# A fused WKV, attention and expert kernel: how gates, q and k travel, where v's bias is added, and which step does what

## The reference

```python
tf = sigmoid(sum(time_emb))                       # per batch
# bi-directional WKV along the tokens, as a gate on a hidden state
h1 = bi_wkv(r=x, k=fside, v=fside, w, u, tf)
qkv = h1 @ Wqkv.T + bqkv                          # 16 heads of 16 channels
a = softmax(q @ k.T * scale) @ v
x1 = x + a @ Wproj.T + bproj
h2 = bi_wkv(r=x1, k=fside, v=fside, w2, u2, tf)   # same scans, second decay
score = sigmoid(h2 @ gate_w.T)                    # 64 experts in 8 groups
# best 4 groups, best 6 experts, weights normalised, times 2.5
y = sum_e gate_e * (relu(h2 @ w1_e.T) ** 2) @ w2_e.T
out = x1 + y + (relu(h2 @ shared_up.T) ** 2) @ shared_down.T
```

## Time and profile before

| | us |
|---|---|
| median of 3 runs | 625.95 (624.86 to 629.41) |
| the profiled execution | 627.93 |
| its span on the core | 626.1 |
| TensorE busy in it | 400.3 (64%), granted clock 0.793 on average |
| VectorE, ScalarE, GpSimd busy | 310.4, 203.9, 129.6 |

### The profile page before, as it was taken

How to read it: one execution, slowest core, us unless ns; L and a number is a source line. 1 busy time by engine, 2 the same in 40 slices (tenths; PEclk the granted TensorE clock), 3 DMA queues, 4 the chain that set the end, 5 groups by cost and what they waited for, 6 DMA issues and landing times.

```text
span 626.1 us, 5613 instructions
## 1 busy us (share of the span) xinstructions
PE 400.3 (64%) x1580; PEld 287.2 (46%) x1580; DVE 310.4 (50%) x552; ACT 203.9 (33%) x392; POOL 129.6 (21%) x117
## 2 busy tenths in 40 slices
PE   0526877688725646768985866672756566576664
PEld 0315554555514435546764654451444444454442
DVE  7779566663462332445653538532433434344343
ACT  3224325533503222244652523321232322323232
POOL 5164315120101010123221221210211212112121
PEclk9957567969657777778998976778878878778889
DMA  7792355142670121212322222222222222232221
GB/s 190 105 169 35 35 67 69 22 49 32 130 111 17 60 93 64 75 56 76 105 79 92 78 94 79 93 71 71 93 90 81 78 93 93 78 92 78 92 97 70
DMA packets 33952, 50.91 MB, mean 81 GB/s; under 512 B 3146, under 2 KB 15626, under 8 KB 33930
## 3 DMA queue, kind: packets, MB, share of 16 engines
q1 hardware_dynamic: 33930, 50.65, 33.1%
HBM read 39.16 MB, written 1.33 MB: 65 GB/s over the span
## 4 chain that ended last, share of the span: by engine, by line
DMA 30%; SPq 28%; PE 18%; DVE 11%; issue 7%; ACT 3%; POOL 1%; DVEq 0%; ACTq 0%; POOLq 0%
SPq L305 20%; DMA ex<-gates 17%; SPq L309 5%; DMA q_st<-nmax_lo 5%; DMA clip<-in_tiles 4%; DMA k_st<-qk_lo 3%; PE ps L1188 3%; PE ps L1243 3%; SPq L343 2%; DVE mx L867 2%; DVE scan L814 2%; DVE t_lo L1019 2%; DVE scan L1098 2%; SPq L351 2%; PE ps L1211 2%
## 5 line engine op out<-in xcount | busy, mean ns | idle before, releaser
L483 POOL TENSOR_TENSOR scan<-scan 128x512 f32<-128x512 f32 x68 | 72.8, 1071 | 372.9 <-ACT scan L647 361.0
L1321 PE MATMUL ps<-hid_hi,t_hi 128*128 128x512 f32 x136 | 71.0, 522 | 91.2 <-DVE t_lo L1019 91.2
L1103 DVE TENSOR_TENSOR qk_lo<-scan,qk_hi 128x512 fp32r<-128x512 f32 x68 | 70.4, 1036 | 70.3 <-ACT qk_hi L657 69.4
L1019 DVE TENSOR_TENSOR t_lo<-clip,t_hi 128x512 fp32r<-128x512 f32 x68 | 47.5, 699 | 102.8 <-ACT t_hi L637 102.7
L637 ACT ACTIVATE t_hi<-clip 128x512 fp32r<-128x512 f32 x68 | 42.6, 627 | 155.3 <-DMA clip<-in_tiles 140.4
L1321 PEld LDWEIGHTS ps<-hid_hi,t_hi 128*128 128x128 f32 x136 | 31.0, 228 | 117.6 <-DVE t_lo L1019 59.1
L1098 DVE TENSOR_TENSOR scan<-scan,ex 128x512 f32<-128x512 f32 x68 | 49.5, 728 | 64.6 <-DMA ex<-gates 42.9
L1211 PE MATMUL ps<-k_st,q_st 96*128 96x256 f32 x128 | 37.2, 384 | 61.5 <-DVE mx L867 53.8
L1332 PE MATMUL ps<-qk_hi,t_hi 128*128 128x512 f32 x136 | 64.3, 473 | 7.4 <-DVE qk_lo L1103 7.3
L1323 PE MATMUL ps<-hid_hi,t_lo 128*128 128x512 f32 x136 | 65.4, 481 | 0.0
L1322 PE MATMUL ps<-hid_lo,t_hi 128*128 128x512 f32 x136 | 64.7, 476 | 0.0
(11 more groups left out here) (123 smaller groups left out, 495.1 us busy)
## 6 DMA issues: line engine op xcount, KB each, us to landing
clip<-in_tiles SPq DMA_DIRECT2D x68, 256.0 KB, 14.6
ex<-gates SPq DMA_DIRECT2D x68, 256.0 KB
q_st<-qk_hi SPq DMA_DIRECT2D x16, 128.0 KB, 3.9
q_st<-qk_lo SPq DMA_DIRECT2D x16, 128.0 KB, 4.9
k_st<-qk_hi SPq DMA_DIRECT2D x16, 128.0 KB, 5.9
k_st<-qk_lo SPq DMA_DIRECT2D x16, 128.0 KB, 6.6
f_sb<-in_fT SPq DMA_DIRECT2D x4, 256.0 KB, 8.6
x_sb<-in_xT SPq DMA_DIRECT2D x4, 256.0 KB, 9.4
```

The costliest lines, as they stand in the source:

```text
L483: g.tensor_tensor(sq[:, k], relu[:, k], relu[:, k], ALU.mult).then_inc(sq_ready, 1)
L1103: TT(act_lo[:, k], act[:, k], act_hi[:, k].bitcast(F32), ALU.subtract).then_inc(act_lo_ready, 1)
L1321: mm(bank_h(bank), w_hi, x_hi, start=(c == 0), stop=False)
```

## The change

1. **Gates.** The spread of a unit's two gate rows is two transfers, one for each row and 64 partitions, instead of one whose source is [2, 64, 512].
2. **q and k.** For batches 1 to 3, `store_qk` writes `qk_hi` and `qk_lo` to DRAM (four transfers of 256 KB a batch), and `load_stack` reads the stacks from there: two of 32 rows for q, four of 16 rows for k, in rows of 8 KB. The evacuation of batches 2 and 3 waits for the stores instead of the stacks.
3. **v's bias** goes through the output projection: before the loop TensorE multiplies it by the output weights (`project_bias`, eight matmuls of one column), and the sum with the projection's bias is what `residual` adds. The output weights are loaded earlier.
4. **Steps.** q and k are projected half at a step over two steps (q 1 and 2; k 4 and 5, in batch 2 5 and 6), v over steps 11 and 12 (12 and 13); `hidden1` is at step 0, the scans follow one step earlier; the tails of batches 0 and 1 begin two and one steps later; the first gates of the router are computed at step 10 and at step 0 of the second loop, and it runs at steps 1 to 4. `GAP` is 2, so every unit from 2 on comes one step later. `jobs` is reordered to match.

```diff
-GAP = 1
+GAP = 2
...
+    qk_dram = nc.dram_tensor("qk_split", (2, B, KC, 2, HD, HB * S), F32, kind="Internal").ap()
...
         def values_at(g):
-            return [n // 4 for n in range(3, H * B, 4) if head_slot(n) + 1 == g]
+            return [n // 4 for n in range(3, H * B, 4) if head_slot(n) + (2 if n in (H + 7,) or n == 7 else 1) == g]
 
         def tail_slot(b):
-            return head_slot(H * b + H - 1) + 2
+            return head_slot(H * b + H - 1) + (4, 3, 2, 2)[b]
...
-            sp.dma_start(bvb[:], bv.partition_broadcast(P)).then_inc(ld_w, 16)
+            sp.dma_start(wo[:], w_out).then_inc(ld_wo, 16)
+            sp.dma_start(bvs[:], bv.rearrange("(c p) -> p c", p=P), allow_slow_non_contiguous=True).then_inc(ld_wo, 16)
...
             def load_spread(half, t, k):
 
-                sp.dma_start(spread[:, k], gates[t, :, half * HT:(half + 1) * HT].unsqueeze(1).broadcast_to([2, P // 2, HT])
-                             ).then_inc(ld_spread[k], 16)
+                for r in range(2):
+                    sp.dma_start(spread[r * (P // 2):(r + 1) * (P // 2), k],
+                                 gates[t, r, half * HT:(half + 1) * HT].unsqueeze(0).broadcast_to([P // 2, HT])
+                                 ).then_inc(ld_spread[k], 16)
...
+            def store_qk(b):
+
+                for w in range(2):
+                    for n, (part, ready) in enumerate(((qk_hi, qk_hi_ready), (qk_lo, qk_lo_ready))):
+                        sp.wait_ge(ready, 4 * b + 2 * w + 2)
+                        sp.dma_start(qk_dram[w, b, :, n].rearrange("t d (h s) -> (d h) t s", s=S),
+                                     part[:, w].bitcast(F32)).then_inc(st_qk[w], 16)
+
...
                 for w in range(2):
+                    if b > 0:
+                        sp.wait_ge(st_qk[w], 32 * b)
+                        src = qk_dram[w, b, half]
+                        width = STACK // (2, 4)[w]
+                        for r in range(0, STACK, width):
+                            rows = src.rearrange("n d s -> (n d) s") if w == 0 else src[r // (STACK // 2)]
+                            sp.dma_start((q_st, k_st)[w][r:r + width, n].rearrange("p h s -> p (h s)").bitcast(F32),
+                                         rows).then_inc(ld_stack[n], 16)
+                        continue
...
             for b in range(B - 1):
+                store_qk(b + 1)
                 load_rows(b, 0)
                 load_stack(b + 1, 0)
...
             def evacuate_qk(b, w):
-                if b > 0:
+                if b == 1:
                     for half in range(KC):
-                        sc.wait_ge(ld_stack[slot(b - 1, half)], 128 * turn(b - 1, half))
+                        sc.wait_ge(ld_stack[slot(0, half)], stacked(0, half))
+                if b > 1:
+                    sc.wait_ge(st_qk[w], 32 * (b - 1))
...
-                    if name == "v":
-                        last = mm(job_bank(job)[:, t * S:(t + 1) * S], k_st[MAXROW:MAXROW + 1, 0, 0, 0:P].bitcast(F32),
-                                  bvb[MAXROW:MAXROW + 1, :], start=False, stop=True, skip_group_check=True)
...
+            def project_bias():
+
+                pe.wait_ge(ld_wo, 32)
+                for t in range(KC):
+                    for c in range(KC):
+                        last = mm(ps[:, 4, S + t:S + t + 1], wo[:, c, t * P:(t + 1) * P], bvs[:, c:c + 1],
+                                  start=(c == 0 and t == 0), stop=(c == KC - 1), skip_group_check=True)
+                last.then_inc(bias_ready, 1)
...
-                if s == 2:
-                    project(b + 1, "q")
+                if s in (1, 2):
+                    project(b + 1, "q", s - 1)
                 if s == 3:
                     subtract_high(b + 1, 0)
-                if s == 4:
-                    project(b + 1, "k")
+                if s - (4, 4, 5)[b] in (0, 1):
+                    project(b + 1, "k", s - (4, 4, 5)[b])
...
+                if s - (11, 11, 12)[b] in (0, 1):
+                    project(b + 1, "v", s - (11, 11, 12)[b])
```

More of the change, by code:

```diff
@@ L81, in bass_adaln_attn_ffn @@
         gw = sb("gw", [P, KC, E])
-        bvb = sb("bvb", [P, C])
+        bias = sb("bias", [P, KC])
+        bvs = sb("bvs", [P, KC])
         gbb = sb("gbb", [P, E])
@@ L170, in bass_adaln_attn_ffn @@
         fill_ready, ld_fill = sem("fill_ready"), sem("ld_fill")
+        st_qk = [sem(f"st_qk{w}") for w in range(2)]
         ld_stack = [sem(f"ld_stack{n}") for n in range(SLOTS)]
@@ L258, in unit_bank, with stacked @@
             return n % 2 if n >= ALONE else 1
+        def stacked(b, half):
+            return 96 * turn(b, half) + (32 if slot(b, half) < 2 else 0)
         def unit_at(s):
@@ L388, in _ @@
                 next_spread(n, 0, n, n % RING)
-            for s in range(HB - 1, HEAD + 1):
-                if s + 1 >= 2 * RING and s + 1 < HEAD:
-                    n = s + 1
+            for s in range(HB - 1, HEAD + 2):
+                n = s + RING + 2 - ENTRY - GAP
+                if 2 * RING <= n < HEAD:
                     next_raw(n, n % NT, n % RING)
-                n = s - 1
+                n = s + RING - ENTRY - GAP
                 if n == NT + SHARED:
@@ L652, in round_act @@
                 if isinstance(n, int) and n == 0:
-                    for half in range(KC):
-                        sc.wait_ge(ld_stack[slot(B - 1, half)], 128 * turn(B - 1, half))
+                    for w in range(2):
+                        sc.wait_ge(st_qk[w], 32 * (B - 1))
                 if not isinstance(n, int) or n >= 2:
@@ L1044, in _ @@
             num_den(1, 0, 1)
+            dve.wait_ge(bias_ready, 1)
+            TT(bias[:], ps[:, 4, S:S + KC], vec[:, V_BP:V_BP + KC], ALU.add).then_inc(bias_sum, 1)
             for g in range(H * (B - 1)):
@@ L1303, in _ @@
             pe.wait_ge(ld_fill, 48)
-            project(0, "v")
+            for t in range(KC):
+                project(0, "v", t)
+            def project_bias():
+                pe.wait_ge(ld_wo, 32)
+                for t in range(KC):
+                    for c in range(KC):
+                        last = mm(ps[:, 4, S + t:S + t + 1], wo[:, c, t * P:(t + 1) * P], bvs[:, c:c + 1],
+                                  start=(c == 0 and t == 0), stop=(c == KC - 1), skip_group_check=True)
+                last.then_inc(bias_ready, 1)
+            project_bias()
             def up(n, half, k, s):
@@ L1368, in _ @@
                         project_out(c)
-                    if t == 8 and c == 1:
-                        gate(c)
-                if s == 15:
-                    turn_max(b, 1)
             for s in range(HEAD + ENTRY + GAP):
@@ L1379, in _ @@
                     scores(B - 1, s + 1)
-                if s == 4:
+                if s == 0:
+                    gate(1)
+                if s == 5:
                     turn_weights(0)
```

90 lines of the change are left out of this document (45 added, 45 removed).

## The result

| | before | after |
|---|---|---|
| median | 625.4 us (621.85 to 629.41, 4 runs) | **444.23 us** (442.77 to 445.36, 4 runs) |
| profiled execution, its span | 627.93, 626.1 us | 445.36, 443.6 us |
| TensorE busy, mean granted clock | 400.3 us (64%), 0.793 | 338.1 us (76%), 0.865 |

The ratio is 0.71, with a 95% interval of 0.7051 to 0.715. Forecast were 446 us and a range of 425 to 505. Runs over 1.5% above the fastest of their kernel are slow ones, and medians leave them out: one of six in e5 (457.33 us), two of six in e9 (455.8 and 457.17).

The account below looks back on a forecast made before the run. The prediction took the gate spread, confined to two DMA engines by its outer size of 2, as the bound. Terms -140 -8 -9 -4.5 -4 -3 -12 = -180.5 us took the 626.1 us span to 445.6, forecast 446 us, range 425 to 505.

Parts of the forecast that it names:

- main term: Feed-forward units from 301 us on: gates in two transfers bring a unit from 5.93 to 2.9 us, -140 us.
- the spread's 6.4 us: Gate spread before the change: 128 packets on two engines, 64 x 0.100 us, taken as the bound of a unit.
- rows of maxima: Transfers of 8 KB at 170, 228 and 289 us: landing sooner saves 8, 9 and 4.5 us.
- q and k through DRAM: Attention loop: half of the 15.9 us that q's evacuation waits for stacks is saved, -8 us; added transfers stay hidden.
- v's bias: Attention loop: two one-row products a batch fall away, 4 us of TensorE over three batches, all counted, -4 us.
- Projections over two steps: Attention loop: together with v's steps and later tails, evens out TensorE's bursts for 0 us (-3 to +4).
- GAP: Steps before unit 2: one more without a unit moves a unit from 7 us steps into 3 us ones, -3 us.
- VectorE's need of 2.38 us a unit: Units in the fast stretch: 3.04 us less 0.66 us idle, so VectorE is no bound.
- Rival 1: Units: the pair of transfers paces them at 3.4 us or more, 473 us, up to 505; chance 0.15.
- Rival 2: Gate spread: the two halves serialise, units stay at 5.93 us, about 614 us; chance 0.05.
- rival 4: Gate spread: one engine handles a one-row source, 12.8 us a unit, near 930 us; chance 0.02.
- rival 3: Units: TensorE falls back to half clock, up to 5.5 us a unit, 586 us; chance 0.04.

Follow-up runs that it names:

- e5: The changed kernel with q's and k's stacks copied from SBUF again, their evacuation waiting for the stacks of the batch before: 451.41 us.
- e9: The changed kernel with both halves of each q, k and v projection at one step again, the second of its two: 450.71 us.
- e3: The changed kernel with the spread's two transfers cut along the tokens, so that each keeps outer size 2: 607.53 us.
- e4: The changed kernel with the spread as one transfer of outer size 64, source [64, 2, 512], hidden channels reordered to suit: 445.04 us.
- e1: The kernel before with the gate spread alone changed to two transfers, one for each gate row: 462.9 us.
- e11: The changed kernel without the router's second pass except its last product; batches 2 and 3 get the gates of 0 and 1: 435.6 us.
- e10: e1 with q and k through DRAM as well, on the old steps and with the old bias: 453.79 us.
- e6: The changed kernel with v's bias added by one-row matmuls in v's projection again: 444.91 us.
- e7: The changed kernel with GAP = 1, so one step without a unit instead of two: 445.36 us.
- e8: The changed kernel without the product of high weights and low hidden state in "up", ten matmuls a unit instead of twelve: 424.47 us.
- e2: The changed kernel with the gate spread as one transfer with source [2, 64, 512] again: 589.48 us.

## Why the prediction was right, and which terms were mis-sized

**The mechanism and the main term held.** e3 and e4 show the outer size as the cause, e1 shows that the terms put down to it (-140 -8 -9 -4.5 -4 = -165.5) came to -165.9 (-163.5 by the spans of the profiled executions). That it fits so closely is in part luck. Within them:
- Units 13 to 67: predicted -140, measured -144.8. The rate is 2.80 us, the lower bound, not 2.9 (54 x 2.80 = 151), and the extras came to 20 us against 19. The second router costs 8.6 of them (9.5 in the profiled execution), where 7 was said (e11).
- Two packets in flight fit the two engines (counted under e4), and the spread's 6.4 us was a little high: it came from the mean of all packets, 0.100 us. Those that run two at a time take 0.088, so 64 of them are 5.6 us of the 6.05 of a unit.
- In e1, with the old steps, the pieces in which the rows of maxima lay gave 5.0 at 170 us (said 8), 7 at 228 (said 9) and 4.5 at 289 (said 4.5), and the one with the first gates gave 2 (said 4). Between units 5 and 10 another 2.5 came, for which the prediction had no term, and up to 165 us 2.3 were lost. The rows and the gates were sized a little high, the gain in the rate a little low.

**q and k through DRAM**: -8 said, -7.2 (e5) and -9.1 (e10) measured. Half of the 15.9 us of the earlier trace rows was the right share, and for the reason given: the projection comes next (e10). The transfers it adds hid, as argued: no wait of TensorE for a stack is among the chain's larger items.

**v's bias**: -4 said, -0.7 measured, which isn't told from nothing. The step that failed is "all counted": the 3.2 us saved up to batch 3 are lost again between units 2 and 10, where the changed kernel has a granted clock of 0.81 and e6 0.88. The prediction counted TensorE's work and left its clock out.

**Projections over two steps**: 0 said, -6.5 measured (e9). This is the largest miss. "Even out TensorE's bursts" was seen and priced at nothing, though the projection's end is what ScalarE waits for next once the stacks are gone. The bound of -3 was too tight as well. The granted clock of the attention loop rose from 0.71 before to 0.80 after (41 to 150 us), but e9 has 0.81 there, so this gain is the shorter wait and not the clock.

**GAP**: -3 said, nothing that can be told measured (e7, 1.1 us).

The attention loop as a whole gave -15.4 against -12, the stretch from unit 0 to 13 gave -14.4 against -20.5, and that behind it 4.8 more than said. These offset, so 446 against 444.23 flatters the working: single terms missed by up to 7 us.

**Signs to look for.** Tile loads at 0.34 us, period 2.80, clock 1.00, DMA share 0.58, rows of maxima in 1.8 us (median of the eight), no wait for stacks, the bump of the router: all as said. One reading carries less far than it seems: VectorE's need of 2.38 us a unit. It holds in the changed kernel (75.54 us busy for 32 units, 2.36), but it isn't fixed. In e8, with the units packed closer, the low split takes 1.35 us instead of 1.18 and the need is 2.64 us, so VectorE is only 0.16 us from being the bound.

**Rivals.** Rival 1 (the pair paces at 3.4 us) is refuted by 187 GB/s without starvation, and 199 in e8. Rival 2 (halves serialise) and rival 4 (one row, one engine) are refuted by the rate itself, and rival 3 by the clock of 1.00.

## What to carry to other kernels

When an issuing engine takes microseconds to hand over a transfer while the DMA share is far below one, look at the outermost size of the transfers in that queue: size 2 gave 84 GB/s, 64 gave 184 with the same bytes. When such a bound falls, list what it had covered (here a router pass, 8.6 us) and which in-order engine now stands behind which wait; moving one group of instructions behind another was worth 31.7 us more. When a burst is "evened out", price the wait of its consumer rather than nothing. And a saving in one stretch can be lost in a later one at a lower granted clock (e6).

## What the runs showed of the hardware that wasn't expected

- A confined transfer harms its neighbours more than its own duration tells. Beside a spread of outer size 2, tile loads of 256 KB had a median of 14.6 us to landing before, 13.6 in e2 and 8.6 in e3; beside one of outer size 64 the median was 2.9 (e4).
- VectorE's subtraction of 128x512 float32 (line 1135) has no fixed price: 0.68 us where GpSimd was idle, mostly 1.11 to 1.23 where it began inside GpSimd's square, up to 1.35 in e8. The price goes by the overlap: duration less the time that the square still ran is 0.55 us in either kernel, and that time is mostly 0.56 to 0.68 us in the changed kernel and up to 0.80 in e8. Two timeline rows of the changed kernel, VectorE and then GpSimd; the subtraction takes 0.68 us where it begins after the square has ended (353.87) and 1.23 where it begins inside one:

```profile
353.93 0.68 DVE L1135 TENSOR_TENSOR qk_lo<-scan,qk_hi 128x512 fp32r<-128x512 f32 x1
...
356.03 1.23 DVE L1135 TENSOR_TENSOR qk_lo<-scan,qk_hi 128x512 fp32r<-128x512 f32 x1 [0.22 <-ACT qk_hi L686]
...
352.83 1.04 POOL L510 TENSOR_TENSOR scan<-scan 128x512 f32<-128x512 f32 x1 [1.78 <-ACT scan L676]
355.56 1.15 POOL L510 TENSOR_TENSOR scan<-scan 128x512 f32<-128x512 f32 x1 [1.68 <-ACT scan L676]
```

- v's bias, 1 KB in pieces of 4 bytes, took 10.3 us to land; it was issued at 5.6 us and first used at 26.7.
